# Third block's path products shared with GpSimd, ScalarE's scaled segments in two PSUM banks, first ReLU in the residual addition

## The reference

```python
x = x + _L0_gnn_ref(_layernorm(x), edge_index, W, b, diffusion_weights)   # relu of a diffusion of x @ W + b
x = x + _L0_ffn_ref(_layernorm(x)[None], ...)[0]                          # 16 gated experts with routing weights
x = x + _L1_gnn_ref(_layernorm(x), edge_attr_512, path_coeffs, src, dst, path_indices)
x = x + _L1_ffn_ref(_layernorm(x)[None], controller, f1, f2)[0]           # permuting mixture of experts
```

## Time and profile before

| what | value |
|---|---|
| median of 3 runs | 277.1 us |
| the profiled execution | 277.36 us, span 275.6 us |
| TensorE busy | 262.8 us, 95% |
| VectorE busy | 223.4 us, 81% |
| ScalarE busy | 168.6 us, 61% |
| GpSimd busy | 39.8 us, 14% |
| granted TensorE clock | 1.00 throughout |

### The profile page before, as it was taken

One profiled execution on the slowest core, in us unless ns is written; L12 is line 12 of the kernel. 1 busy time (PEld: TensorE's weight loads), 2 busy tenths in 40 slices (PEclk: granted clock), 3 DMA queues, 4 the chain that ended last, 5 costly groups with the idle time before them and its releaser, 6 DMA issues.

```text
span 275.6 us, 5667 instructions
## 1 busy us (share of the span) xinstructions
PE 262.8 (95%) x1639; PEld 184.2 (67%) x1639; DVE 223.4 (81%) x660; ACT 168.6 (61%) x341; POOL 39.8 (14%) x52
## 2 busy tenths in 40 slices
PE   6899999999999899998999999969999989999996
PEld 4566598886444699996778786746666654468633
DVE  5977565199757999999999999999999987655372
ACT  6930451011526999988888787499988809352260
POOL 4000060060005766661000000000000000000000
DMA  6699990000013765555342000013444428100002
GB/s 205 229 409 409 446 402 17 0 2 1 1 38 117 197 174 150 168 155 155 84 149 77 2 0 2 2 27 146 159 156 148 150 87 335 39 4 2 2 0 76
DMA packets 12592, 33.91 MB, mean 123 GB/s; under 512 B 3345, under 2 KB 3602, under 8 KB 12306
## 3 DMA queue, kind: packets, MB, share of 16 engines
q1 hardware_dynamic: 10482, 26.73, 26.8%
q0 software_dynamic: 2080, 6.82, 8.7%
HBM read 32.50 MB, written 1.05 MB: 122 GB/s over the span
## 4 chain that ended last, share of the span: by engine, by line
PE 83%; DVE 7%; ACT 4%; issue 2%; DMA 2%; DVEq 1%; ACTq 0%; SPq 0%
PE psum L1285 15%; PE psum L1336 15%; PE psum L1239 10%; PE psum L1339 8%; PE psum L1263 5%; PE psum L1268 4%; PE psum L1291 3%; PE psum L1410 3%; PE psum L1436 3%; PE psum L1182 3%; DVE big L1030 2%; PE psum L1168 2%; PE psum L1327 2%; DMA xs<-in_x 2%; PE psum L1191 1%
## 5 line engine op out<-in xcount | busy, mean ns | idle before, releaser
L1285 PE MATMUL psum<-big,dst_oh 128*128 128x512 f32 x108 | 50.6, 593 | 0.2 <-DVE big L1030 0.2
L604 ACT ACTIVATE prod<-edges,coef_b 128x320 f32 (+1 forms) x78 | 43.7, 594 | 10.9 <-PE psum L1339 9.4
L1336 PE MATMUL psum<-prod,ident 128*128 128x128 f32 x160 | 32.0, 294 | 0.7 <-DVE prod L1020 0.5
L1336 PEld LDWEIGHTS psum<-prod,ident 128*128 128x128 f32 x160 | 24.4, 190 | 10.1 <-issue 9.2
L1020 DVE TENSOR_TENSOR prod<-big,prod 128x320 f32<-128x320 f32 (+1 forms) x53 | 29.0, 549 | 0.2 <-DVE big L991 0.2
L1285 PEld LDWEIGHTS psum<-big,dst_oh 128*128 128x128 f32 x108 | 18.7, 191 | 14.7 <-issue 14.3
L1239 PE MATMUL psum<-edges,big 128*128 128x256 f32 x128 | 28.3, 380 | 0.0
L604 ACT ACTIVATE xparts<-edges,coef_b 128x320 f32 (+1 forms) x48 | 26.0, 591 | 1.2 <-PE psum L1336 0.9
L1239 PEld LDWEIGHTS psum<-edges,big 128*128 128x128 f32 x128 | 24.1, 190 | 3.5 <-issue 0.3
L1030 DVE TENSOR_TENSOR big<-big,prod 128x64 f32 (+2 forms) x80 | 26.2, 328 | 0.2 <-issue 0.2
L469 POOL DMA_INDIRECT big<-xn_rows,big x16 | 17.2, 1076 | 30.3 <-DMA xn_rows<-xn 23.5
(11 more groups left out here) (222 smaller groups left out, 526.3 us busy)
## 6 DMA issues: line engine op xcount, KB each, us to landing
big<-in_w SPq DMA_DIRECT2D x3, 2048.0 KB, 16.2
edges<-in_edge SPq DMA_DIRECT2D x1, 3584.0 KB, 23.9
edges<-in_f SPq DMA_DIRECT2D x7, 512.0 KB, 3.4
edges<-in_edge SPq DMA_DIRECT2D x1, 2560.0 KB, 24.1
edges<-in_edge SPq DMA_DIRECT2D x5, 512.0 KB, 3.6
edges<-in_f SPq DMA_DIRECT2D x1, 2560.0 KB, 10.1
big<-in_f SPq DMA_DIRECT2D x4, 512.0 KB, 3.3
big<-in_gnn_w SPq DMA_DIRECT2D x1, 1024.0 KB, 6.3
```

The costliest lines, as they stand in the source:

```text
L604: nc.scalar.activation(slot(n)[:, 0:BLOCKS[b], :], segment(edges_of(b), single_column(words, p)), ACT.Copy, scale=coef_b[:, p:p + 1]).then ...
L1285: last = mm(bank[2 + h], dst_oh[:, n % DR, h * P:(h + 1) * P], tile_sums(b, t), start=False, stop=False)
L1336: last = mm(path_sums(to), ident[:], product[:, 0:PT].rearrange("p t u -> p (t u)"), start=False, stop=True, skip_group_check=True)
```

## The change

In the third block, for products from path 12 on (`POOLED_FROM`):

- GpSimd adds two of the six tiles that VectorE added (`POOLED`), counted in `pool_sums`, each after its multiply and after its own add before. VectorE's add takes the other four. VectorE's first such add is waited for by GpSimd's first.
- ScalarE writes its scaled segment not into the slot but into bank 0 or 1 of PSUM, by the parity of n. It waits for `mults` at n - 1, that is for the end of multiply(n - 2), in place of the two waits for the slot.
- VectorE's multiply reads that bank and writes the slot. It waits in addition for `psums` and `pool_sums` of product n - 12.
- What waited for the last `sums` waits for the last `pool_sums` too.

At the end of the first block the ReLU instruction is gone. ScalarE multiplies `xs` by the row sums in place (before the diffusion product is there), and VectorE computes max(product, 0) + xs in one instruction from PSUM. `xs` is then too large by the row sum: the root gets the scale `rinv2` = rinv * rinv, `rstd` is multiplied by `rinv` (one more one-column instruction in each half), and the second residual, L972, becomes xs * rinv + product.

```diff
+    POOLED, POOLED_FROM = 2, 12
+    assert KEPT[NB - 1] == PT
...
+        def pooled(n):
+            return n >= NP * (NB - 1) + POOLED_FROM
+
+        def pool_sums_at(n):
+            return max(0, n - NP * (NB - 1) - POOLED_FROM)
+
+        def scaled_at(n):
+            if pooled(n):
+                return bank[n % 2][:, 0:BLOCKS[NB - 1] * U].rearrange("p (t u) -> p t u", u=U)
+            return slot(n)[:, 0:BLOCKS[n // NP], :]
...
+            pool.wait_ge(packed, 3)
+            words = load_words(pool, 0, ROW_PATHS)
+
+            def add_pooled(n):
+                pool.wait_ge(mults, n + 1)
+                if n == NP * (NB - 1) + POOLED_FROM:
+                    pool.wait_ge(sums, n)
+                else:
+                    pool.wait_ge(pool_sums, pool_sums_at(n))
+                v = segment(rest_sums[NB - 1][:, 0:POOLED, :], out_column(words, n % NP))
+                nc.gpsimd.tensor_tensor(v, v, slot(n)[:, PT:PT + POOLED, :], ALU.add).then_inc(pool_sums, 1)
+
+            for n in range(NP * (NB - 1) + POOLED_FROM, NP * NB):
+                add_pooled(n)
...
-                nc.scalar.activation(root[:, h:h + 1], mv[:, h, 1:2], ACT.Sqrt, bias=eps[:]).then_inc(root_ready, 1)
+                scale = rinv2[:, h, :] if n == 1 else 1.0
+                nc.scalar.activation(root[:, h:h + 1], mv[:, h, 1:2], ACT.Sqrt, bias=eps[:], scale=scale).then_inc(root_ready, 1)
...
-            act.wait_ge(xnT_a, 2)
-            for h in range(H):
-                act.wait_ge(diff_ps, h + 1)
-                nc.scalar.activation(xn[:, h, :], bank[6 + h], ACT.Relu, scale=rinv[:, h, :]).then_inc(relu_done, 1)
+            act.wait_ge(inv_ready, 1)
+            for h in range(H):
+                nc.scalar.activation(xs[:, h, :], xs[:, h, :], ACT.Copy, scale=rsum[:, h, :]).then_inc(rows_scaled, 1)
...
-                if n >= SLOTS:
+                if pooled(n):
+                    if not pooled(n - 1):
+                        act.wait_ge(block_out, banks_before(NB - 1))
+                    act.wait_ge(mults, n - 1)
+                elif n >= SLOTS:
                     act.wait_ge(psums, n + 1 - SLOTS)
                     act.wait_ge(sums, n + 1 - SLOTS)
-                nc.scalar.activation(slot(n)[:, 0:BLOCKS[b], :],
+                nc.scalar.activation(scaled_at(n),
...
-            def normalise(h, of=xs[:]):
+            def inverse(h, by_rows):
...
                 link(nc.vector.reciprocal(rstd[:, h:h + 1], root[:, h:h + 1]))
+                if by_rows:
+                    link(nc.vector.tensor_tensor(rstd[:, h:h + 1], rstd[:, h:h + 1], rinv[:, h, :], ALU.mult))
...
-            link(nc.vector.reciprocal(rinv, rsum))
+            link(nc.vector.reciprocal(rinv[:], rsum))
+            nc.vector.tensor_tensor(rinv2[:], rinv[:], rinv[:], ALU.mult).then_inc(inv_ready, 1)
...
-                dve.wait_ge(relu_done, h + 1)
-                link(nc.vector.tensor_tensor(xs[:, h, :], xs[:, h, :], xn[:, h, :], ALU.add))
+                dve.wait_ge(rows_scaled, h + 1)
+                dve.wait_ge(diff_ps, h + 1)
+                link(nc.vector.scalar_tensor_tensor(out=xs[:, h, :], in0=bank[6 + h], scalar=0.0, in1=xs[:, h, :],
+                                                    op0=ALU.max, op1=ALU.add))
                 if h:
-                    centre()
+                    centre(True)
                 variance(h)
-            normalise(1)
+            normalise(1, by_rows=True)
...
-                nc.vector.tensor_tensor(xs[:, h, :], xs[:, h, :], bank[2 + h], ALU.add).then_inc(x2_ready, 1)
+                nc.vector.scalar_tensor_tensor(out=xs[:, h, :], in0=xs[:, h, :], scalar=rinv[:, h, :], in1=bank[2 + h],
+                                               op0=ALU.mult, op1=ALU.add).then_inc(x2_ready, 1)
...
                 dve.wait_ge(scaled, sum(not direct(*divmod(m, NP)) for m in range(n + 1)))
-                nc.vector.tensor_tensor(v, segment(xg[:, 0:tiles, :], first_column(words[b], p)), v, ALU.mult).then_inc(mults, 1)
+                if pooled(n):
+                    dve.wait_ge(psums, n + 1 - SLOTS)
+                    dve.wait_ge(pool_sums, pool_sums_at(n + 1 - SLOTS))
+                nc.vector.tensor_tensor(v, segment(xg[:, 0:tiles, :], first_column(words[b], p)), scaled_at(n), ALU.mult)\
+                    .then_inc(mults, 1)
...
-                v = segment(rest_sums[b], out_column(words[b], p))
-                nc.vector.tensor_tensor(v, v, slot(n)[:, KEPT[b]:BLOCKS[b], :], ALU.add).then_inc(sums, 1)
+                skip = POOLED if pooled(n) else 0
+                v = segment(rest_sums[b][:, skip:, :], out_column(words[b], p))
+                nc.vector.tensor_tensor(v, v, slot(n)[:, KEPT[b] + skip:BLOCKS[b], :], ALU.add).then_inc(sums, 1)
```

More of the change, by code:

```diff
@@ L135, in graph_and_experts @@
         root = sb("root", [P, H + 1])
+        rinv = sb("rinv", [P, H, 1])
+        rinv2 = sb("rinv2", [P, H, 1])
         eps = sb("eps", [P, 1])
@@ L195, in graph_and_experts @@
         rsum = take([H, 1])
-        rinv = take([H, 1])
         w0sum = take([H, 1])
@@ L736, in normalise, with centre @@
                 link(nc.vector.reciprocal(rstd[:, h:h + 1], root[:, h:h + 1]))
+                if by_rows:
+                    link(nc.vector.tensor_tensor(rstd[:, h:h + 1], rstd[:, h:h + 1], rinv[:, h, :], ALU.mult))
+            def normalise(h, of=xs[:], by_rows=False):
+                inverse(h, by_rows)
                 nc.vector.tensor_scalar(xn[:, h, :], of[:, h, :], mv[:, h, 0:1], rstd[:, h:h + 1],
                                         ALU.subtract, ALU.mult).then_inc(xn_ready, 1)
[L740 to L744 removed]
+            def centre(by_rows=False):
+                inverse(0, by_rows)
                 nc.vector.scalar_tensor_tensor(out=shift[:], in0=mv[:, 0, 0:1], scalar=-1.0, in1=rstd[:, 0:1],
```

10 lines of the change are left out of this document (5 added, 5 removed).

## The result

The changed kernel took 280.3 us in the median of four runs (279.46, 279.46, 281.15, 281.16), the kernel before 277.11 on the same chip: ratio 1.0115, 95% interval 1.0097 to 1.0133. No single run took the median: two took 279.46, two 281.15 and 281.16, and 280.3 lies between the pairs. The forecast was 278.9 in a range of 276.6 to 282.5, slower with a chance of 0.71. The profiled execution of the changed kernel took 281.15, its span is 279.2 (275.6 before).

A forecast was written before the change was run, and what follows sets the result against it. TensorE was taken as busiest and on the chain nearly everywhere, with VectorE near its limit in the third block. Terms 1.8 + 0.2 - 0.13 - 0.1 = +1.8 on the median 277.1 gave 278.9 us, range 276.6 to 282.5.

The forecast's parts named there:

- The ring of two banks: Third block from path 12: ScalarE and VectorE wait on each other's bank, 1.42 per two paths, +1.8 us; own range 277.5 to 280.8.
- the one-hots: Third block: twelve one-hot copies in ScalarE's queue between scalings of paths 15 to 62, +0.2 us, ends 0 and +0.6.
- ScalarE's access to PSUM: Third block: scaling into PSUM instead of SBUF takes 0.52 instead of 0.56, one access moved being worth 0.035.
- its 0.755 per path: Third block: pace by the Trainium skill's access times, a turn of 1.51 for two paths, costing some 4 us.
- GpSimd is hidden: Third block: GpSimd's adds, 0.30 each at a pace of 0.59, end before VectorE's own last add and cost nothing.
- the cover: Third block: GpSimd's pace of 0.59 stays below 0.71 per path; gone if one add takes over 0.42.
- the third rival: Third block: GpSimd sets the pace, at 0.50 per add a turn of 0.79; 280.5 to 285 us, chance 0.19.
- TensorE as the next floor: End of third block's path loop: VectorE's end can come at most some 1.6 us earlier before TensorE takes over.
- One sign: Third block: TensorE short of work from about 200 on, as a sign that the predicted slower pace holds.
- The end of the loop: Third block: last multiply's start to last add's end falls from 1.30 to 1.17, -0.13 us.
- The first residual: End of first block: ReLU removed from the chain, second half's normalised rows 0.19 earlier; sum -0.1 us, ends -0.46 and +0.2.
- The 0.08 for the squared reciprocal: First block: the new rinv squared on VectorE ahead of cmat costs some 0.08 on TensorE's chain.

## Why the prediction was right, and where it was off

- **The ring of two banks sets the pace: right.** The kernel with the banks alone and no work for GpSimd has the changed kernel's pace. The turn was predicted at 1.42 and measured at 1.459: multiply 0.488 (0.48), first handoff 0.207 (0.20), scaling 0.529 (0.52), second handoff 0.235 (0.22). Those means hold the one-hots, for which the forecast had a term of its own, so its 1.42 is to be held against the median turn, 1.445: too small by 0.025, 0.6 us over 51 paths. What the means add to the median, 0.25 us over the 51, stands for the one-hots (0.2 forecast) and the two long waits. The third block's pace was to cost 2.0 and cost 2.6. The handoffs, read from other pairs of engines, held to 0.01 in the median.
- **ScalarE's access to PSUM: right in kind.** The saving taken from one row of another instruction was 0.035 and came to 0.026 (0.555 to 0.529 in the mean). The multiply from PSUM takes 0.472 to 0.490 in all traces that have it; from SBUF it takes 0.483 in the kernel before: no surcharge. The Trainium skill (Perfetto Trace Analysis, Optimizing Scalar/DVE Operations) has one for VectorE and none is seen here; its 0.755 per path was too high.
- **GpSimd is hidden: right in the changed kernel, and only with the banks.** Its add takes 0.32 undisturbed (0.30 forecast) and 0.37 to 0.47 beside an add of VectorE, which no term had; its turn is 0.63 where it follows itself at once, not 0.59, since the handoff to itself is 0.31. Eight of the 52 took over 0.42, where the cover was said to be gone, and it held: they come in turn with shorter ones, and GpSimd never falls more than a path behind. Half of the third rival's mechanism is real: with the segments in SBUF the two engines hold each other up and the pace is 0.731. The other half, GpSimd's chain with multiplies waiting for it, is not seen even there: no multiply waits, VectorE's own instructions are longer. In the changed kernel the multiply, with an operand in PSUM, keeps its length, and so do VectorE's adds (0.28 to 0.29), though GpSimd's grow where the two meet. The Trainium skill (SBUF — State Buffer, Who interferes with whom) names this condition, and the traces agree in kind: multiplies of two SBUF operands are lengthened, those with one in PSUM are not. The lengthening, 0.13, is well under the 0.32 that waiting out a whole add would make.
- **TensorE as the next floor: right.** The cap was put at 1.6 us. With two tiles' sums left out the tail came 2.0 earlier, and the chain there is TensorE's alone. One sign failed: TensorE was to be short of work from about 200 on, but in the changed kernel it is busy in all 20 us from 196 to 216, 3.93 and 3.94 of each four up to 224, and 3.31 of the next four.
- **The end of the loop: right**, -0.13 forecast and -0.13 measured.
- **The first residual: right, a little better.** The second half's statistics were forecast at 31.80 against 32.26; they start at 31.55 in an execution whose diffusion matmuls came 0.25 earlier, so exactly there. From them to the transposes it was to be 0.27 longer and is 0.29 (2.35 against 2.06; the root with a pointer scale takes 0.39 instead of 0.29). That leaves -0.17. The 0.08 for the squared reciprocal ahead of the diffusion does not stand out of the half microsecond by which its start varies.
- **Not foreseen: the clock.** The measured median is 1.4 above the forecast. That it lies in the range, and even in the ring's own 277.5 to 280.8, is in part luck: the upper two runs lie outside the latter, and the range's upper end was made for a rival that was not in force. The lower two runs (279.46) are 0.6 above it, the ring's 0.6. The upper two are 1.7 higher, and the profiled one of them has a stretch at half clock on the tail's first matmuls. The trace of before had no such stretch at all, so no row spoke of it. Whether the changed kernel draws it on more often than the kernel before is open: 3 of its 9 runs are the longer kind, and 4 of 83 of the kernel before.

## What to carry to other kernels

Before moving work off an engine, ask what the next one can do: VectorE here had 1.6 to 2 us to give before TensorE took over, so a change with a ring of its own could hardly win. A ring of two buffers between two engines costs both engines' instructions plus two handoffs of 0.2 us every second turn; unless that is well under the present pace, make it three deep, which took the loss back here and brought no gain. And price an engine's help with the helper running: where GpSimd's adds met instructions of VectorE with both inputs in SBUF, both grew by a quarter to a half, which gave back what the adds had saved.

## What was unexpected of the hardware

- An add of GpSimd and an instruction of VectorE with two SBUF operands lengthen each other in the kernel with GpSimd's adds alone (0.32 to 0.42; the multiply from 0.48 to 0.61, the add of four tiles from 0.28 to 0.41, one of the two in each path). The same multiply with one operand in PSUM runs beside GpSimd at 0.472 to 0.490. In the changed kernel only GpSimd's side grows where the two adds meet, to as much as 0.47, and VectorE's stays at 0.28 to 0.29 (in the second trace of this kernel with one exception, 0.45).
- GpSimd's add of 32 columns takes 0.25, of 64 columns 0.32: by these two, some 0.18 of it does not depend on the size.
- Stretches of 3.4 us at half of TensorE's clock come in traces of every batch, in nearly the same kernel at other places. Early in the third block they cost nothing that shows: the kernel with the banks alone has 6.8 us of it from 185.6, that with GpSimd's adds alone none there, and both need 47.45 to the tail. On the tail's first matmuls one costs 1.7 us (7.08 instead of 5.39), and was seen there in two of fourteen profiled executions.
